# Stores of x issued elsewhere, and other engine orders in the final stage of a gated cross-attention network

## The reference

```python
# layer 2, feed-forward: a mixture of 8 experts, the best 2 for each row (token)
probs = softmax(x_flat @ router_w.T); top_v, top_i = top_k(probs, 2)
# rows are gathered per expert (capacity 640), then
h = gelu(expert_in @ w1[e]); y = h @ w2[e]
out += y[slot] * gate            # back to the row, gate from top_v
x = x + tanh(g_ffn[2]) * out
# layer 3, attention
att = softmax(Q @ K.T / 16); X = layer_norm(Q + att @ V)
X2 = layer_norm(relu(X @ W1 + b1) @ W2 + b2 + X)
x = x + tanh(g_xattn[3]) * X2    # Q = layernorm(x), K = V = context
# layer 3, feed-forward: weights by their sign
y = clip((layernorm(x) @ sign(w).T) * scale + bias, -100, 100)
x = x + tanh(g_ffn[3]) * y
```

## Time and profile before

| | us |
|---|---|
| median of 3 runs | 966.32 (965.63 to 971.49) |
| profiled execution | 968.61 |
| its span, first to last instruction | 966.7 |
| TensorE busy | 836.3 (87%) |
| VectorE busy | 631.3 (65%) |
| GpSimd busy | 538.5 (56%) |
| ScalarE busy | 527.4 (55%) |

### The profile page before, as it was taken

The page is one execution under the profiler, slowest core; times in us unless marked ns, Lnnn a source line. Parts: engine busy times, 40 slices in busy tenths (PEclk is TensorE's granted clock), DMA queues, the critical chain, the costliest instruction groups (busy, mean ns, idle before and its releaser), DMA issues.

```text
span 966.7 us, 18422 instructions
## 1 busy us (share of the span) xinstructions
PE 836.3 (87%) x5646; PEld 679.4 (70%) x5646; DVE 631.3 (65%) x2700; ACT 527.4 (55%) x1290; POOL 538.5 (56%) x743
## 2 busy tenths in 40 slices
PE   6899999997774776778687889999999999998895
PEld 5677767884443444545466679999999999977773
DVE  3877766889988999999997742222222222426784
ACT  3777755689875878889777312122122122226762
POOL 2566445585553877777664035545545545237882
PEclk9999999998897676879998789999999999999998
DMA  9100001000000090000000952222222222130001
GB/s 291 41 2 2 1 2 44 1 1 1 1 1 1 21 372 1 1 12 13 12 13 4 356 176 36 37 40 38 35 39 38 35 40 33 23 99 1 16 30 44
DMA packets 37963, 47.20 MB, mean 49 GB/s; under 512 B 4438, under 2 KB 33854, under 8 KB 37867
## 3 DMA queue, kind: packets, MB, share of 16 engines
q1 hardware_dynamic: 29131, 35.77, 10.9%
q0 software_dynamic: 8736, 10.25, 6.7%
HBM read 34.46 MB, written 11.55 MB: 48 GB/s over the span
## 4 chain that ended last, share of the span: by engine, by line
PE 57%; DVE 26%; POOL 6%; issue 5%; ACT 5%; DMA 2%; SPq 0%; POOLq 0%; DVEq 0%; ACTq 0%
PE ps L2605 15%; PE ps L2616 14%; DVE experts L1587 4%; DVE experts L1597 4%; PE ps L2111 3%; DVE m8b L1592 3%; PE ps L2134 3%; DVE m L1582 3%; PE ps L2029 3%; PE ps L2098 2%; DVE mx L1577 2%; PE ps L2121 2%; DVE sm L1515 2%; PE ps L2058 1%; PE ps L2238 1%
## 5 line engine op out<-in xcount | busy, mean ns | idle before, releaser
L1846 DVE COPY ptall<-experts 128x512 f32 x156 | 60.0, 425 | 152.1 <-PE ps L2605 147.2
L2605 PE MATMUL ps<-xnT,ptall 128*128 128x128 f32 x1248 | 148.3, 278 | 0.0
L2605 PEld LDWEIGHTS ps<-xnT,ptall 128*128 128x128 f32 x1248 | 145.2, 195 | 0.1
L2616 PE MATMUL ps<-experts,wk 128*128 x624 | 141.2, 379 | 1.4 <-ACT xkeep L1203 1.4
L2616 PEld LDWEIGHTS ps<-experts,wk 128*128 128x128 f32 x624 | 115.6, 190 | 15.9 <-issue 1.8
L1194 ACT ACTIVATE wk<-ps 128x1024 f32<-128x1024 f32 x39 | 39.9, 1024 | 154.3 <-PE ps L2605 154.3
L734 POOL DMA_INDIRECT xn<-expert_in,rown x39 | 38.5, 987 | 131.1 <-PE ps L2593 104.3
L1078 ACT ACTIVATE experts<-experts,mcol 128x77 f32<-128x77 f32 x256 | 87.9, 351 | 0.1
L750 POOL DMA_INDIRECT token_sum<-xkeep,dest x39 | 64.3, 1648 | 35.5 <-ACT xkeep L1203 25.4
L2029 PE MATMUL ps<-ones 128*128 128x256 bf16 x436 | 59.5, 297 | 5.8 <-POOL mone L517 5.8
L559 POOL TENSOR_TENSOR experts<-experts,rden 128x616 f32<-128x616 f32 x32 | 38.8, 1216 | 46.1 <-DVE rden L1372 46.1
(11 more groups left out here) (324 smaller groups left out, 2100.1 us busy)
## 6 DMA issues: line engine op xcount, KB each, us to landing
experts<-in_ew SPq DMA_DIRECT2D x16, 1024.0 KB, 12.0
x<-in_x SPq DMA_DIRECT2D x1, 2048.0 KB, 10.9
xkeep<-in_bw SPq DMA_DIRECT2D x2, 1024.0 KB, 7.2
expert_in<-xkeep SPq DMA_DIRECT2D x8, 256.0 KB
token_sum<-x SPq DMA_DIRECT2D x1, 2048.0 KB
x<-token_sum SPq DMA_DIRECT2D x8, 256.0 KB, 4.4
out<-x SPq DMA_DIRECT2D x8, 256.0 KB, 2.1
xn<-expert_in,rown POOLq DMA_INDIRECT x39
```

What stands on the lines that cost most here:

```text
L1846: ins = nc.vector.tensor_copy(tilew[:, v, c, :], experts[:, bass.ds(e * EW + (c * FF + v * 512), 512)])
L2605: ins = nc.tensor.matmul(ps[j % 2][:, v, k * P:(k + 1) * P], tilew[:, v, c, k * P:(k + 1) * P], xTb[j % 3][:, c, :], start=c == 0, stop=c ...
L2616: ins = nc.tensor.matmul(bank(4)[:, 0:D], hidT[j % 2][:, k * P:(k + 1) * P], experts[:, bass.ds(e * EW + (E * EW + k * D), D)], start=k == ...
```

## The change

`KEPT` and `STORES` count what SP has stored. Before, all of x went to `token_sum` in one store of 2 MB and one of 128 KB (the spare rows), behind the stores of normalized rows and all expert weights. Now batches 0 to 3 are stored one at a time behind `stored(b)` (`base_rows`), the spare rows behind them, and batches 4 to 7 in one store of 1 MB after TensorE has turned the rows of the first two tiles (`m_xp` at 2), ahead of the store of the gates. GpSimd's wait before the first gather is for the stores of normalized rows, of batches 0 to 3 and of the spare rows. In the final stage the lists of all four compute engines are in another order, with other batch numbers, and TensorE has `warm(110, 0)` in step B + 4, ahead of the transposes of the last batch.

```diff
--- before.py
+++ after.py
@@ -271,7 +271,8 @@
         xs_d = nc.dram_tensor("expert_in", [TT * P, D], f32).ap()
         acc_d = nc.dram_tensor("token_sum", [B * S + P, D], f32).ap()
         gate_d = nc.dram_tensor("token_gates", [P * 2 * TT, 1], f32).ap()
-        STORES = (B + 3) * 16
+        KEPT = (B + B // 2 + 1) * 16
+        STORES = KEPT + 2 * 16
 
         def landed(j):
 
@@ -472,9 +473,15 @@
                     sp.dma_start(xs_d[b * S:(b + 1) * S, :].rearrange("(t p) d -> p t d", p=P),
                                  xkeep[:, TB * b:TB * b + TB, :]).then_inc(s_kd, 16)
 
+                def base_rows(first, last):
+                    sp.dma_start(acc_d[first * S:last * S, :].rearrange("(t p) d -> p t d", p=P),
+                                 x[:, TB * first:TB * last, :]).then_inc(s_kd, 16)
+
                 second(0)
                 for b in range(B // 2):
                     stored(b)
+                    base_rows(b, b + 1)
+                sp.dma_start(acc_d[B * S:B * S + P, :], x[:, 0, :]).then_inc(s_kd, 16)
                 sp.wait_ge(done[4].sem, done[4].past(TT))
                 for e in range(1, 5):
                     second(e)
@@ -482,15 +489,15 @@
                     stored(b)
                 for e in range(5, E):
                     second(e)
-                sp.wait_ge(s_kd, B * 16)
-                sp.dma_start(acc_d[0:B * S, :].rearrange("(t p) d -> p t d", p=P), x[:, :, :]).then_inc(s_kd, 16)
-                sp.dma_start(acc_d[B * S:B * S + P, :], x[:, 0, :]).then_inc(s_kd, 16)
+                sp.wait_ge(s_kd, KEPT)
                 sp.wait_ge(xtp[5].sem, xtp[5].past(B))
                 for w, key in ((w3a, "w3a"), (w3b, "w3b"), (w3f, "w3f")):
                     sp.dma_start(w, a[key].rearrange("(c p) n -> p c n", p=P)).then_inc(s_w[7], 16)
                 sp.dma_start(bc3, a["bc3"].partition_broadcast(P)).then_inc(s_w[7], 16)
                 sp.dma_start(xkeep[:, 13:14, :], a["b2"].partition_broadcast(P)).then_inc(s_w[7], 16)
 
+                sp.wait_ge(m_xp.sem, m_xp.past(2))
+                base_rows(B // 2, B)
                 sp.wait_ge(rt_v.sem, rt_v.past(GATED))
                 sp.dma_start(gate_d.rearrange("(p n) o -> p (n o)", p=P), gsent).then_inc(s_kd, 16)
                 for u in range(3):
@@ -725,7 +732,7 @@
                 for b in range(B // 2 + 1, B):
                     l5_scale(b)
             if phases >= 6:
-                gp.wait_ge(s_kd, B * 16)
+                gp.wait_ge(s_kd, KEPT)
                 gp.wait_ge(keep_s.sem, keep_s.past(B))
                 gp.wait_ge(inv_s.sem, inv_s.past(1))
                 for j in range(MT + 6):
@@ -764,18 +771,18 @@
 
             gp.wait_ge(g7, 2)
             for k in range(B + 5):
+                if 0 <= k - 3 < B:
+                    post_scale(k - 3, 1e-6, mv_a, rs_a, nm_a, xa7, za7, ra7, B)
                 if k < B:
                     post_scale(k, 1e-5, mv, rs_l, nm_l, c7, n7, r7, B)
                 if 0 <= k - 5 < B:
                     post_scale(k - 5, 1e-5, mv_e, rs_e, nm_e, c8, n8, r8, B)
+                if 0 <= k - 2 < B:
+                    post_beta(k - 2)
                 if 0 <= k - 4 < B:
                     post_scale(k - 4, 1e-6, mv_b, rs_b, nm_b, yb7, zb7, rb7, B)
                 if 0 <= k - 3 < B:
                     post_scaled(k - 3)
-                if 0 <= k - 2 < B:
-                    post_scale(k - 2, 1e-6, mv_a, rs_a, nm_a, xa7, za7, ra7, B)
-                if 0 <= k - 1 < B:
-                    post_beta(k - 1)
 
 
 
@@ -1285,7 +1292,17 @@
                     ac.wait_ge(pv7, B + b - 1)
                 copy(pt[p][:, 0:S], bank(1)[0:KEYS, S:2 * S]).then_inc(pt7, 1)
 
-            for k in range(B + 5):
+            for k in range(B + 6):
+                if 0 <= k - 2 < B:
+                    post_probs(k - 2)
+                if 0 <= k - 3 < B:
+                    post_norma(k - 3)
+                if 0 <= k - 6 < B:
+                    post_turned8(k - 6)
+                if 0 <= k - 3 < B:
+                    post_turned(k - 3)
+                if 0 <= k - 5 < B:
+                    post_norm8(k - 5)
                 if k < B:
                     post_norm7(k)
                 if 0 <= k - 1 < B:
@@ -1294,18 +1311,8 @@
                     post_normb(k - 4)
                 if 0 <= k - 3 < B:
                     post_relu(k - 3)
-                if 0 <= k - 5 < B:
-                    post_turned8(k - 5)
-                if 0 <= k - 1 < B:
-                    post_probs(k - 1)
                 if k < B:
                     post_turned7(k)
-                if 0 <= k - 2 < B:
-                    post_norma(k - 2)
-                if 0 <= k - 2 < B:
-                    post_turned(k - 2)
-                if 0 <= k - 4 < B:
-                    post_norm8(k - 4)
 
 
 
@@ -1995,26 +2002,25 @@
                 ve.wait_ge(own_v.sem, n)
                 nc.vector.scalar_tensor_tensor(two, ye, gates[:, 7:8], two, ALU.mult, ALU.add).then_inc(d8, 1)
 
-            for k in range(B + 7):
-                if 0 <= k - 5 < B:
-                    post_sums(k - 5)
-                    post_statsb(k - 5)
+            for k in range(B + 8):
+                if 0 <= k - 6 < B:
+                    post_sums(k - 6)
+                    post_statsb(k - 6)
+                if 0 <= k - 4 < B:
+                    post_values(k - 4)
                 if 0 <= k - 3 < B:
-                    post_values(k - 3)
-                if 0 <= k - 2 < B:
-                    post_soft(k - 2)
+                    post_soft(k - 3)
+                if 0 <= k - 4 < B:
+                    post_statsa(k - 4)
+                if 0 <= k - 8 < B:
+                    post_out(k - 8)
                 if 0 <= k - 3 < B:
-                    post_statsa(k - 3)
+                    post_sum(k - 3)
                 if k < B:
                     post_stats7(k)
-                if 0 <= k - 7 < B:
-                    post_out(k - 7)
-                if 0 <= k - 5 < B:
-                    post_gated(k - 5)
-                if 0 <= k - 2 < B:
-                    post_sum(k - 2)
-                if 0 <= k - 5 < B:
-                    post_stats8(k - 5)
+                if 0 <= k - 6 < B:
+                    post_gated(k - 6)
+                    post_stats8(k - 6)
 
 
 
@@ -2720,28 +2726,30 @@
 
             warm(100, 7)
             for k in range(B + 5):
+                if k == B + 4:
+                    warm(110, 0)
+                if 0 <= k - 5 < B:
+                    post_flip8(k - 5)
                 if k < B:
                     post_flip7(k)
+                if 0 <= k - 1 < B:
+                    post_flipp(k - 1)
                 if 0 <= k - 3 < B:
                     post_second(k - 3)
                 if 0 <= k - 1 < B:
                     post_values(k - 1)
                 if k < 3:
                     warm(6, 7)
+                if 0 <= k - 2 < B:
+                    post_flipx(k - 2)
                 if k < B:
                     post_scores(k)
-                if 0 <= k - 2 < B:
-                    post_flipx(k - 2)
                 if 0 <= k - 5 < B:
                     post_last(k - 5)
                 if 0 <= k - 2 < B:
                     post_first(k - 2)
                 if k < 3:
                     warm(10, 7)
-                if k < B:
-                    post_flipp(k)
-                if 0 <= k - 4 < B:
-                    post_flip8(k - 4)
 
 
 def kernel(**inputs):
```

## The result

The changed kernel takes 971.51 us (median of 7 runs, 969.47 to 973.19), the kernel before beside it 967.83. The ratio is 1.0044, 95% interval 1.0025 to 1.0063: 4.3 us slower. That is little, but the interval lies clear of 1. The profiled execution took 971.19 us, with a span of 969.3, 2.6 more than before.

What follows compares the result with a forecast made beforehand. Bounds: gather waits and half clock at the expert head; GpSimd in mid final stage, TensorE after about 920 us. Sum 968.61 - 2.5 + 0 + 6.8 = 972.9 us profiled, 970.6 median; range 962 to 977.5.

Steps and rivals of the forecast that it cites:

- the head: Start of the expert part: moving 2.2 MB of stores lets first products start at 564.1, not 566.57; 2.5 us gained.
- A gather: Row gathers at the expert part's start: each put at 3.0 us from issue start, landing at 561.2 and 562.7.
- a sign of being wrong: Start of the expert part: a first set of products starting before 563 or after 566 would show the prediction wrong.
- the case in which it falls: First set of expert products: TensorE's clock falls all the same, set takes 6.1 us; 2.5 us gained.
- the other end: First set of expert products: clock keeps 2.4 GHz, set takes 3.6 us; 5.0 us gained; chance 0.14.
- The first half of the stores: Stores of batches 0 to 3 and spare rows, issued by SP well before 530 us: cost nothing.
- The second half and the gate store: Expert part: 1 MB store takes SP 1.5 us, gate store issued 565.6, GpSimd goes on at 569.6; costs nothing.
- The third rival: Expert part: no gain, gate store lands 2.5 us or more after 571.7 or gathers meet 1 MB; 973.1; chance 0.08.
- New orders: Final stage: reordered engine lists put at 0, between 3 us gained and a loss given as a rival.
- The fourth rival: Final stage: VectorE's products delay GpSimd 1.5 us more in each of five rounds, 7.7 in all; 978.3; chance 0.07.
- Constant products: End of final stage: 110 take 12.0 us, cover 3.06, last turn 9.0 us late; 6.8 lost in sum.
- The 2.1 us given back: Last product of the final stage: runs at full clock, 2.1 us instead of 4.2.

Runs made afterwards that it cites:

- e6: Stores of x moved, old orders, the 50 constant products ahead of the expert part left out, against the kernel before: 966.11 us, ratio 1.0022.
- e3: Kernel before with only the 110 constant products ahead of the last transposes added: 976.58 us, ratio 1.0126 to the kernel before.
- e4: Kernel before with only the new orders of the final stage, stores unmoved, no drain products: 965.85 us, ratio 1.0024 to the kernel before.
- e11: Kernel before with stores of x moved and 110 constant products added, old orders: 971.96 us, ratio 1.0060 to the kernel before.
- e2: Kernel before with only the stores of x moved: 960.8 us, ratio 0.9961 to the kernel before.
- e7: Kernel before with only batches 0 to 3 and spare rows stored early, the other 1 MB issued at the old place: 964.95 us, ratio 0.9994.
- e5: Kernel before, stores unmoved, with 48 instead of 20 constant products before the first gather is needed: 967.0 us, ratio 1.0012.

## Why the prediction was right, and where it was off

Bound of the kernel, and the head. The wait went, and VectorE's weight copy was the next one late, as said: 2.5 us forecast, 2.8 measured (its copy starts 0.28 us sooner behind the routing than before). A gather was put at 3.0 us; it took at most 3.15 here, and 3.5 in e6, where TensorE stood waiting for it. The Trainium skill, "DMA: Bandwidth & Descriptors", section "Anatomy of one DMA", gave an estimate of 2.3 for it; e6's measurement is 1.2 longer, and it decides. The first set started at 562.38, before the 563 that was named as a sign of being wrong. But this trace is 1.2 us early: on the clock of before it is 563.6, against 564.1 forecast.

The clock at the head. I took the case in which it falls, by the nearest row, and named 5.0 us as the other end. It held in all eight profiles with the full move and the products ahead: 5.3 us against the profile of before. The term was too small by 2.8 us against that profile. In the median the head is worth 3.8. A likely reason is that the kernel before often loses less in its first set than it did in its profile (4.5 and 4.6 in e3 and e4); three profiles don't show how often.

The first half of the stores cost nothing: SP issues them from 418 to 505 us in 0.47 to 0.49 us each. The second half and the gate store: GpSimd was to go on at 569.6, and did at 568.40, in a trace that is 1.2 us early: the same moment. It cost nothing. That the moment agrees is luck. The 1 MB store was put at 1.5 us of SP's time, by half of the 3.04 that the 2 MB one took; it took 0.38, so the gate store was issued 1.1 us sooner than forecast (563.26, or 564.4 on the clock of before). Behind the 1 MB it took 5.1 us and not 4.0. The third rival's condition also has a slip: 574.2 is 8.6 us behind the gate store's own forecast issue (565.6), not 7.5.

New orders: 0 forecast, between -3 and 3; a cost of 0.3 to 0.5 in the traces, and not to be told from 0 in the runs. The fourth rival's mechanism shows, in its size it doesn't: 0.4 and 0.25 in two rounds and not 1.5 in five; nor were there five full rounds of 9.9, but three, followed by 8.5 to 8.9. The 0.6 of before was not freed either, it moved to other instructions. The Trainium skill, "SBUF — State Buffer", section "Who interferes with whom", says that a VectorE instruction with two inputs in SBUF contends with a GpSimd instruction that reads SBUF. The two small instructions agree with it, each longer by 0.4, beside products of 0.69.

Constant products: 9.0 forecast for the delay of the last turn, 10.9 measured against the moment at which the batch was ready. The 12.0 us of products are right; their cover was 1.1 us and not 3.06. The product ahead of them ran at half clock, which took 1.7 of it, and the last normalization came 0.5 sooner. The 2.1 us given back at the last product were there against the profile of before, but most profiles without products don't lose them at all.

The sum was 972.9 for the profiled execution, and 971.19 was measured; 970.6 for the median, and 971.51 was measured. As a difference that is 4.3 us forecast (970.6 - 966.3) and 4.3 measured. The mechanisms were right, but an agreement this close is luck. Two terms were too small by 2.8 and by 1.9 us with opposite signs, and the 1.2 us by which the trace was early for another reason did the rest. By the ratios it is the same: the stores gave 3.8 where 2.5 stood in the sum, and the products cost 9.6 (e11 over e2) where 6.8 stood. The rounds of 10.30 lie within the 0.5 that was allowed around 9.9.

## What to carry to other kernels

Constant products that are to hold the clock are free only inside the gap that they fill. Past it each costs its own time (0.109 us here). A gap has to be read from the profile, with the product ahead of it at its slower clock. A transfer that is moved out of a full stretch is worth only as much as the next thing allows to come sooner; look for that on the other engines' timelines before counting bytes. And where a term hangs on the clock, one profile is one draw: look at the same set of products in several.

## What the runs showed of the hardware

The first set of 32 products, which is the same code, took 6.1, 4.5 and 4.6 us in the profiles of before, e3 and e4, where it started 24.3, 24.6 and 24.2 us behind the same mark. At what moment the granted clock falls and comes back differs from execution to execution.

A gather of 128 rows of 1 KB took at most 3.15 us from the start of its issue to TensorE's start, and 3.5 in e6, with nothing of x left ahead of it, 6.0 with 1 MB in front (e7) and 6.4 with 2 MB (before). A store of 16 KB landed, by the moment at which GpSimd went on, 3.9 us behind its issue with nearly empty queues in before and 2.2 in e5, 5.1 behind 1 MB, and 7.7 behind 3 MB (574.12 - 566.41).
